# Layer 0's attention opened by the rows of x, with native float32 projections and stacks filled from SBUF

## The reference, cut to what matters

```python
xn = layernorm(x)                               # [8, 128, 512]
Q = (xn @ Wq + bq)      # 32 heads of 16        -> [8, 8, 4, 128, 16]
K = (ctx @ Wk + bk)     # 8 key heads of 16     -> [8, 8, 128, 16]
V = (ctx @ Wv + bv)
scores = einsum('bhgqd,bhkd->bhgqk', Q, K) / 4
w = softmax(scores)
y = einsum('bhgqk,bhkd->bhgqd', w, V)           # back to [8, 128, 512]
x = x + y @ Wo + bo
```

## Time and profile before

| | us |
|---|---|
| median of 3 runs | 1290.59 |
| the profiled execution | 1297.16 |
| its span in the trace | 1295.9 |
| TensorE (PE) busy | 1212.4 (94%) |
| VectorE (DVE) busy | 836.0 (65%) |
| ScalarE (ACT) busy | 690.2 (53%) |
| GpSimd (POOL) busy | 415.8 (32%) |
| first product on TensorE | 11.10 |
| first query product | 32.50 |
| first score product | 64.85 |
| first turned score product | 85.62 |
| last turned score product | 204.1 |

### The profile page before, as it was taken

How to read it: one execution, slowest core, us unless ns; L and a number is a source line. 1 busy time by engine, 2 the same in 40 slices (tenths; PEclk the granted TensorE clock), 3 DMA queues, 4 the chain that set the end, 5 groups by cost and what they waited for, 6 DMA issues and landing times.

```text
span 1295.9 us, 16380 instructions
## 1 busy us (share of the span) xinstructions
PE 1212.4 (94%) x5860; PEld 946.8 (73%) x5860; DVE 836.0 (65%) x1547; ACT 690.2 (53%) x1575; POOL 415.8 (32%) x486
## 2 busy tenths in 40 slices
PE   4979887989999999989999999998999999999997
PEld 4756554656676676768888888877888888888765
DVE  5546665776776678475566666784446666667756
ACT  3235454337777778435555555672345555566621
POOL 5341120066777677101232223240022232323200
PEclk8979998999999999989999999999999999999998
DMA  7464430178667967622111121220302121211101
GB/s 246 146 200 111 143 119 33 40 266 271 106 125 198 265 146 145 165 88 65 58 58 65 44 63 47 60 82 26 96 26 65 58 65 58 65 42 49 57 1 65
DMA packets 73985, 130.49 MB, mean 101 GB/s; under 512 B 11376, under 2 KB 30704, under 8 KB 71344
## 3 DMA queue, kind: packets, MB, share of 16 engines
q1 hardware_dynamic: 55584, 80.91, 20.0%
q0 software_dynamic: 18320, 48.52, 15.1%
HBM read 150.37 MB, written 29.10 MB: 138 GB/s over the span
## 4 chain that ended last, share of the span: by engine, by line
PE 71%; DVE 10%; DMA 6%; issue 5%; POOL 4%; ACT 3%; SPq 0%; POOLq 0%; ACTq 0%; DVEq 0%
PE bank L451 54%; PE bank L1969 7%; PE bank L1945 4%; DMA moe<-ys,token_out 3%; POOL moe L1545 2%; PE bank L635 2%; DVE rden L841 1%; POOL xs L1534 1%; PE bank L2284 1%; DMA q0st<-m0T 1%; DVE xn L422 1%; PE bank L1221 1%; DVE stats L397 1%; PE bank L622 1%; PE bank L607 1%
## 5 line engine op out<-in xcount | busy, mean ns | idle before, releaser
L1937 POOL TENSOR_SCALAR p<-p,mx 128x256 f32<-128x256 f32 x256 | 162.8, 652 | 524.5 <-DVE mx L1931 524.5
L1130 DVE TENSOR_TENSOR wf_lo<-wf_raw,wf_hi 128x512 fp32r<-128x512 f32 x192 | 124.4, 689 | 37.6 <-ACT wf_hi L1124 33.0
L1923 ACT ACTIVATE p<-bank,mx 128x256 f32<-128x256 f32 x256 | 118.0, 485 | 10.7 <-DVE mx L1913 10.6
L451 PE MATMUL bank<-xnA_hi,w1q_hi 128*128 128x512 f32 x288 | 118.8, 412 | 3.6 <-DVE xnA_lo L445 3.2
L1124 ACT ACTIVATE wf_hi<-wf_raw 128x512 fp32r<-128x512 f32 x192 | 110.1, 625 | 11.5 <-DMA wf_raw<-in_wffn,weight_row 11.5
L451 PE MATMUL bank<-xnA_hi,w1q_lo 128*128 128x512 f32 x288 | 114.8, 399 | 0.0
L451 PE MATMUL bank<-xnA_lo,w1q_hi 128*128 128x512 f32 x288 | 114.2, 397 | 0.0
L1952 ACT ACTIVATE p1T_hi<-bank 128x512 fp32r<-128x512 f32 x128 | 75.1, 596 | 65.7 <-PE bank L1945 65.7
L1877 ACT ACTIVATE q1T_hi<-bank 128x512 fp32r<-128x512 f32 x64 | 38.2, 597 | 132.6 <-PE bank L451 132.6
L451 PE MATMUL bank<-w1o_hi,a1T_hi 128*128 128x512 f32 x256 | 105.2, 411 | 0.1
L451 PE MATMUL bank<-wf_raw,zT 128*128 128x512 f32 x220 | 102.9, 593 | 2.2 <-DVE x L1204 1.3
(11 more groups left out here) (337 smaller groups left out, 3129.3 us busy)
## 6 DMA issues: line engine op xcount, KB each, us to landing
w_raw<-in_wq SPq DMA_DIRECT2D x64, 256.0 KB
w_raw<-in_wo SPq DMA_DIRECT2D x64, 256.0 KB
q0st<-q_rows SPq DMA_DIRECT2D x8, 768.0 KB, 5.5
moe<-xn SPq DMA_DIRECT2D x2, 2304.0 KB, 14.0
q_rows<-q0T_hi SPq DMA_DIRECT2D x16, 256.0 KB
returned<-moe SPq DMA_DIRECT2D x8, 512.0 KB, 7.3
k0bd<-k_rows SPq DMA_DIRECT2D x16, 192.0 KB, 5.9
x<-in_x SPq DMA_DIRECT2D x8, 256.0 KB, 6.8
```

Of the source, the lines that this page charges most:

```text
L451: ins = nc.tensor.matmul(ps, a, b, start=(n == 0), stop=(n == len(pairs) - 1))
L1130: nc.vector.tensor_tensor(wf[m % 2][1][:, a, c, :], raw[m % STREAMS][:, a, c, :], wf[m % 2][0][:, a, c, :].bitcast(F32), ALU.subtract).the ...
L1923: ins = nc.scalar.activation(pr1[s % 2][:, h, :], banks.of(("s1", s, n))[:, hh * 2 * P:(hh + 1) * 2 * P], ACT.Exp, bias=m[:, UH + h:UH + h ...
L1937: ins = nc.gpsimd.tensor_scalar(pr1[s % 2][:, h, :], pr1[s % 2][:, h, :], m[:, 3 * UH + h:3 * UH + h + 1], 1.0, ALU.mult, ALU.mult)
```

## The change

The loads come in another order: the first four tiles of x, Wq, Wk, half 0's context, and then the rest. Context, Wq, Wk, Wv and the normalised rows of layer 0 are no longer split: their products run in native float32 (one product in place of three). Wq's and Wk's columns are permuted by ACT as it copies them (`query_weight` and the copy into wk), so that in q0T the 8 partitions of a dimension group and in k0T the 16 partitions of all heads of a dimension lie such that a stack's rows can be filled by one transfer from SBUF. The DRAM buffers q_rows and k_rows are gone. For each batch `queries_in` issues 12 transfers of 64 KB (4 groups m by 3 row sets, 8 partitions each), `keys_in` 6 of 64 KB (16 partitions each), and `maxima` 4 of 8 KB, now on SP instead of GpSimd. The rings are three of k0bd and four of q0st. All four query groups of half 1 stand among the units (QUERY_STEPS), half 1's values and keys in the first ten steps (`opening_steps`). GpSimd no longer makes Wq's low half; ACT splits Wo between half 0's query groups. Zeros for the fill of moe are written later (batch 6 instead of 4), and GpSimd's table `upto` waits for the last turned score.

The queries of half 0 stand ahead of keys and values, and those of half 1 (the last four rows) behind the first turned score. The diff, cut to its core:

```diff
+        q0T = pair("q0T", [P, KT, HT])
+        qst23 = [sb(f"q0st{i}", [P, KV0, 2, P], F32R) for i in (2, 3)]
+        ctxT = [sb(f"ctx0_{i}", [P, KT, HT]) for i in range(2)]
+        wq = sb("wq0", [P, KT, D])
+        wkv = sb("wkv0", [P, 2, KT, P])
+        wk = sb("wk0", [P, KT, P])
...
             act.wait_ge(S["xn_turned"], t + 1)
+            if g < 2:
+                nc.scalar.activation(xnF[g][:, :, k * P:(k + 1) * P], ps3,
+                                     ACT.Copy).then_inc(S["xn_ready"], 1)
+                return
...
+        QUERY_STEPS = (-1, 3, 6, 9)
...
             def keys_in(b):
-                sp.wait_ge(S["st_k"], 48 * (half + 1))
+                sp.wait_ge(S["kbd_set"], b % KRING + 1)
+                sp.wait_ge(S["k0_lo"], half + 1)
                 if b >= KRING:
                     sp.wait_ge(S["t0_mm"], KV0 * (b - KRING + 1))
                 for h in range(2):
+                    for c in range(3):
+                        row = QROWS // 2 * h + HD0 * c
+                        load(kbd[b % KRING][row:row + HD0, :, h, :].bitcast(F32),
+                             k0T[half][STACK_K[c]][:, tok].bitcast(F32)).then_inc(S[f"ld_k0{b % KRING}"], 16)
+            def queries_in(b, m):
+                sp.wait_ge(S["q0_lo"], half * KT + m + 1)
+                if b >= RING0:
+                    sp.wait_ge(S["t0_mm"], KV0 * (b - RING0 + 1))
+                for c in range(3):
+                    row = QROWS // 2 * (m // 2) + HD0 * c + HD0 // 2 * (m % 2)
+                    load(qst[b % RING0][row:row + HD0 // 2, :, :, :].bitcast(F32).rearrange("p k j t -> p (k j) t"),
+                         q0T[STACK_Q[c]][:, m, tok].bitcast(F32)).then_inc(S[f"ld_q0{b % RING0}"], 16)
...
+            for m in range(KT):
+                if m == 2:
+                    keys_in(0)
+                    queries_in(3, 0)
+                for b in range(3):
+                    queries_in(b, m)
+            keys_in(1)
+            keys_in(2)
+            maxima(0)
+            for m in range(1, KT):
+                queries_in(3, m)
+            for b in range(1, B):
+                maxima(b)
+                if b + 2 < B:
+                    keys_in(b + 2)
+                if b + 3 < B:
+                    for m in range(KT):
+                        queries_in(b + 3, m)
...
+        def opening_steps(i, turn, values, keys, query, maxima):
+            j = i + LEAD_S
+            if j in (1, 2):
+                turn(j + 1)
+            if j == KV0 - 1:
+                maxima()
+            if HB <= j < B:
+                values(j)
+            if j == KV0 + 1:
+                keys()
+            if i in QUERY_STEPS:
+                query(QUERY_STEPS.index(i))
...
-                mm_group(ps[:, :], [q for k in range(KT) for q in three(
-                    (wq[0][:, k, cols], wq[1][:, k, cols]),
-                    (xnA[0][:, k, :], xnA[1][:, k, :]))]).then_inc(S["q0_mm"], 1)
+                mm_group(ps[:, :], [(wq[:, k, m * P:(m + 1) * P], xnF[half][:, k, :])
+                                    for k in range(KT)]).then_inc(S["q0_mm"], 1)
...
             def query(half, m):
                 act.wait_ge(S["q0_mm"], half * KT + m + 1)
                 if half:
-                    act.wait_ge(S["st_q"], 48 * KT)
+                    for b in range(HB):
+                        act.wait_ge(S[f"ld_q0{b}"], 192)
+            def query_weight(k):
+                act.wait_ge(S["ld_wq0"], 16)
+                nc.scalar.activation(wq[:, k, :].rearrange("p (h d g) -> p h d g", h=2, d=HD0),
+                                     w_raw[:, k, :].rearrange("p (g h d) -> p h d g", h=2, d=HD0),
+                                     ACT.Copy).then_inc(S["wq0"], 1)
...
+            pool.wait_ge(S["t0_mm"], UNITS0)
             nc.gpsimd.iota(upto[:, :, :], [[1, E0], [-1, E0]], base=0, channel_multiplier=0,
```

More of the change, by code:

```diff
@@ new lines, in maxima @@
+            def maxima(b):
+                half = H0 // 2
+                sp.wait_ge(S["m0_lo"], b + 1)
+                for q in range(2):
+                    for h in range(2):
+                        row = QROWS + 2 * q + h
+                        load(qst[b % RING0][row:row + 1, :, :, :].bitcast(F32).rearrange("p k j t -> p (k j) t"),
+                             mT[b % 2][h * half:(h + 1) * half, q, :].bitcast(F32)).then_inc(
+                                 S[f"ld_m0{b % RING0}"], 16)
@@ L582, in values @@
-            def values(b, ring):
-                ps = banks.take(next(ring), ("v0", b), (S["v0"], b + 1))
-                pe.wait_ge(S["ctx0_lo"], KT * (b // HB + 1))
-                pe.wait_ge(S["wkv0_lo"], 2)
-                cols = slice((b % HB) * P, (b % HB + 1) * P)
-                mm_group(ps[:, 0:P], [q for k in range(KT) for q in three(
-                    (ctxT[0][:, k, cols], ctxT[1][:, k, cols]),
-                    (wkv[0][:, 1, k, :], wkv[1][:, 1, k, :]))]).then_inc(S["v0_mm"], 1)
@@ L591, in query, with keys @@
[L591 to L598 removed]
+            def keys(half, n):
+                ps = banks.take(n, ("k0", half), (S["k0_lo"], half + 1))
+                pe.wait_ge(S["wk0"], 1)
+                pe.wait_ge(S[f"ld_ctx0{half}"], 16)
+                mm_group(ps[:, :], [(wk[:, k, :], ctxT[half][:, k, :])
+                                    for k in range(KT)]).then_inc(S["k0_mm"], 1)
@@ L668, in tensor_attention0 @@
                     turned_scores(i + LEAD_T)
-                before_steps(i, lambda m: query(1, m, fill), lambda: maxima(0))
+                opening_steps(i, lambda k: norm_turn(1, k, next(fill)), lambda v: values(v, next(fill)),
+                              lambda: keys(1, next(fill)), lambda m: query(1, m, next(yrs)), lambda: maxima(0))
                 if 0 <= i < UNITS0:
@@ L781, in scalar_attention0 @@
                     softmax_exp(i + LEAD_T)
-                before_steps(i, lambda m: query(1, m), lambda: maxima(0))
+                opening_steps(i, lambda k: norm_hi(1, k), nothing, lambda: keys(1), lambda m: query(1, m),
+                              lambda: maxima(0))
                 b = of_batch(i, LEAD_S)
@@ L915, in vector_attention0 @@
                     softmax_max(i + LEAD_S)
-                before_steps(i, lambda m: query(1, m), lambda: maxima(0))
+                opening_steps(i, nothing, values, lambda: keys(1), lambda m: query(1, m), lambda: maxima(0))
                 b = of_batch(i, LEAD_S)
```

366 lines of the change are left out of this document (126 added, 240 removed).

## The result

| | before | changed |
|---|---|---|
| median of 20 runs each | 1291.17 us | 1297.01 us |
| profiled execution | 1297.16 us, span 1295.9 | 1301.11 us, span 1299.8 |
| moved by the DMA engines | 130.49 MB | 122.67 MB |
| first score product / first turned score | 64.9 / 85.6 us | 60.6 / 75.7 us |
| last turned score | 204.1 us | 211.3 us |

The changed kernel is slower by 0.33%: the ratio on record is 1.0033, with a 95% interval from 1.0018 to 1.0049 (the two medians alone lie 5.8 us, 0.45%, apart). The forecast was 1281.2. The profiled execution of the changed kernel is the slowest of its twenty (1288.82 to 1301.11). The work of layer 0 did start earlier, but by 9.9 us instead of 23.2 at the first turned score, and 17.1 us came back between the first and the last one.

A forecast was written before the change was run, and what follows sets the result against it. Layer 0's opening was taken to be limited by SP's queue of stack pieces. First turned score 23.2 us earlier, less 13.8 for queries among the units, gives -9.4 us, hence 1281.2 us; range 1268 to 1297.

The forecast's parts named there:

- the drain of the pieces in the DMA engines: Opening's query pieces: eight engines at 14 GB/s each pass 64 KB in 0.57 us, giving 0.60 us with SP's row.
- SP's first piece: Opening, SP's queue: the first stack piece can go at 19.5 + 0.69 + 0.75 = 21.0 us.
- First tile: Opening: first normalised tile at 8.5 us instead of 22.64, with the table load ahead of any data.
- first query product: Opening, TensorE: starts at 14.3 us instead of 32.50, 18.2 us earlier, with Wq no limit.
- One issue on SP: SP's queue: 0.60 us a piece, bounded by 0.41 and 1.21; 39 transfers ahead of batch 0's last piece take 23.4 us.
- Landing: Opening, batch 0's last stack piece: 2.0 us to land, so that scores can start at 46.4 us.
- From the scores to the first turned score: Opening: scores from 46.4 us, first turned score at 62.4 instead of 85.62, 23.2 us earlier.
- What comes back: Attention units: half 1's four query groups now lie among them and cost TensorE 4 x 3.44 = 13.8 us.
- The balance of idle time: Units: new maxima waits of 4 to 6 us against 7.8 before, counted as nothing, bounded by -4 and +8.
- Batch 3's maxima behind the wf_raw load: Units, SP's queue: these maxima stand behind the 1.5 MB load and come 2 to 4 us late.
- Rival 1: Stack pieces' queue: SP's pieces bound a slower kernel, 1297 at 0.75 us each, 1346 at 1.21; chance 0.20.
- Rival 2: Stack pieces cheap at 0.43 us: scores at 39.8, first turned score at 54, time 1269 us; chance 0.17.

## Why the prediction was wrong

The path was named rightly: statistics first, then SP's queue of pieces, then scores, with the queries of half 1 coming back among the units. The step that failed most is one term of the sum, **the drain of the pieces in the DMA engines**. The prediction took 14 GB/s for an engine from stack loads of before, so that "eight of them pass 64 KB in 0.57 us", and concluded "With the DMA engines and with SP's own row I come out at the same value". Measured are 76 GB/s beside the pieces (26 to 38 us), 64 KB in 0.86 us, and SP's own rows say 0.87 once it is held up. SP issues faster than that before, a backlog grows, and the 2.0 us for landing became 9.64. The row of 14 GB/s was of loads from DRAM into 96 or 48 partitions; with sixteen or every second partition as destination the engines gave 16.3 and 17.5, and landing took 2.3. Both runs gained 7 to 8 us, where the term was short by 7.0.

That term alone doesn't account for the miss: without it the kernel took 1288.1, not 1281.2. Layer 0 ended 7.2 us later instead of 9.4 earlier, 16.6 us off: 7.1 are the landing and the start behind it, 3.5 the start of SP's first piece, 3.6 SP's issues and stalls, 3.3 what the units gave back beyond the forecast, less 0.9 gained between the scores and the first turned score.

- First tile 8.5 forecast, 9.42 measured; first query product 14.3 and 16.27. The table load was not ahead of data (7.58), but Wq decided: it landed at 10.2 us, and then its four copies (1.09 us each) stood between the evictions on ACT until 16.2. The prediction had "a part of a weight copy" in the way.
- SP's first piece 21.0 forecast, 24.48 measured: the 2.0 above, and 1.4 because the four products of the first group took 6.6 us, partly at the lower clock, 5.2 forecast.
- One issue on SP 0.60 forecast, 0.645 measured with the gap between two: 1.7 us over 38, and 1.9 us of stalls on top (the 1.96 of one row). The start of the 39th was 43.8 by the forecast and 50.9 in fact: 3.5 + 1.7 + 1.9.
- Landing: 7.0 us more than the 2.0 and the issue. Scores at 60.6 instead of 46.4, and that is 7.1 + 7.0 and 0.1 to the start of the product.
- From the scores to the first turned score 16.0 forecast, 15.1 measured: right. So the gain there is 9.9 instead of 23.2.
- What comes back: 13.8 for the queries forecast; 17.1 measured. The queries' price was right: the projections' rows (L451) are busy for 14.4 us more between the first and the last turned score (34.6 against 20.2), though all of TensorE's work there is only 10.9 more, at a granted clock of 0.97 instead of 0.95. The idle time was to be even, and is 6.3 us more.
- The balance of idle time had two faults. It set 3.76 and 4.06 us of old waits against the new ones, but these rows are the transfers' time in flight; TensorE stood idle for 2.67 and 2.03 us there, by these rows of the kernel before:

```profile
140.51 0.48 PE L622 MATMUL bank<-q0st,k0bd 100*128 100x256 f32 x2 [2.67 <-DMA q0st<-m0T]
...
174.12 0.47 PE L622 MATMUL bank<-q0st,k0bd 100*128 100x256 f32 x2 [2.03 <-DMA q0st<-m0T]
```

- The same balance took ten of a batch's transfers at 0.5 us. Measured are 0.64 for keys and 0.62 for the maxima's rows, so a batch needs 12 x 0.645 + 6 x 0.64 + 4 x 0.62 + 1.85 = 15.9 us against its 14.9: 1 us late instead of just enough, as the other waits of the maxima show (0.6 to 2.0 us).
- Batch 3's maxima behind the wf_raw load were forecast "2 to 4 us late"; the row at 134.3 has 6.6, and moving that load gained 5.7.
- The value products 0.25 us each forecast, 3.74 / 16 = 0.234 measured: right.
- The layers behind kept 3.9 us of the 7.2 by which layer 0 ended late in these two profiles; the mean granted clock is 0.982 here and 0.977 before. No run took the other 3.3 us apart.

Rival 1, "SP's pieces are the bound and the kernel gets slower", is what happened, at 1297.0 against its 1297, but that the figures meet is luck, since the mechanism was another: it was to decide from 0.70 us of SP and to be late in every batch by that. SP stayed at 0.645 until the engines held it up; the engines took 0.87 a piece, and that cost its 7 us once, in the opening. The upper end of the rival, 1346, is also summed wrongly: at 1.21 us the 45 query pieces of the opening alone take 27 us more, so that it would lose 4 us instead of giving 3, and the sum comes to about 1353. Rival 2's rule, in the Trainium skill (DMA: Bandwidth & Descriptors, "Why small descriptors are slow (HBM only)"), put no penalty on pieces between SBUF and SBUF; here a 512 B packet took 57 or 28 ns by its destination alone. So there is a penalty between SBUF and SBUF too, though it hangs on the destination's partitions; no run varied the size.

## What to carry to other kernels

A transfer cut into small pieces has two prices, the issue on its queue and the drain in the engines, and a drain that is slower shows mainly as a late landing of the last one: read GB/s beside the DMA share, for the very shape of the destination, and take a rate from another shape only as one end of a range. Where many small transfers go from SBUF to SBUF, try spreading the destination over more partitions, even with gaps, first (here 7 to 8 us). Then look at what a queue has ahead of the one transfer that is waited for: a large load there, or pieces that another queue could carry, cost about as much (here 5.7 and 6.8 us).

## What the runs showed of the hardware

- Writes from SBUF to SBUF in 512 B packets (26 to 38 us): into 8 neighbouring partitions 76 GB/s at a DMA share of 0.60; into 8 partitions with gaps 98 at 0.35; into 16 neighbouring ones 107 at 0.41. The last two are bounded by SP. A packet took 57, 28 and 29 ns.
- SP issues such transfers one each 0.645 us, of 64 KB, and 0.62 of 8 KB; behind a full queue of slow pieces one each 0.87. GpSimd issues the 64 KB ones each 0.53 us (a row of four in 2.12).
- ACT copies 512 columns of float32 in 1.09 us when it reads with a stride, as Wq's copy in the changed kernel, and in 0.60 when it doesn't.
- A load of 1.5 MB on the same engines delayed four rows of 8 KB by 5 us (6.75 instead of 1.85 us to land).
